# A selective-state kernel: growth factors and dt's steps in PSUM, C rotated on GpSimd, the MLP sum earlier on VectorE, and the products from the states over all four heads at a time

## What is computed

```python
zxbcdt = x @ in_proj_w.T                        # z, x, B, C and dt; x is layer-normalised first
dt  = softplus(zxbcdt[..., -NHEADS:] + dt_bias)
xBC = silu(causal_conv4(xBC))                   # x_ssm (4 heads x 64), B and C (32 complex each)
theta      = clip(theta_base + tanh(x @ theta_w1) @ theta_w2)
lambda_eff = lambda_base + eta * theta ** 2
log_z  = complex(-lambda_eff * dt, theta * dt)
x_disc = x_ssm * dt
# linear recurrence over time, for every head and state k:
#   S_t = exp(log_z_t) * S_{t-1} + B_t * x_disc_t ;   y_t = Re(sum_k C_t * S_t)
y = y + x_ssm * D
g = rmsnorm(y * silu(z)) * norm_w
out = x + g @ out_proj_w.T + mlp(layernorm(x))  # 128 -> 512 -> 512 -> 128, weights +1 and -1
```

## Time and profile before

| | |
|---|---|
| median of 3 runs | 410.99 us (410.89 to 411.18) |
| profiled execution | 410.37 us, span of its instructions 407.0 us |
| TensorE busy | 334.8 us, 82% |
| VectorE busy | 310.3 us, 76% |
| ScalarE busy | 171.7 us, 42% |
| GpSimd busy | 147.6 us, 36% |
| mean granted TensorE clock | 0.94 of full speed |

### The profile page before, as it was taken

One profiled execution on the slowest core, in us unless ns is written; L12 is line 12 of the kernel. 1 busy time (PEld: TensorE's weight loads), 2 busy tenths in 40 slices (PEclk: granted clock), 3 DMA queues, 4 the chain that ended last, 5 costly groups with the idle time before them and its releaser, 6 DMA issues.

```text
span 407.0 us, 9993 instructions
## 1 busy us (share of the span) xinstructions
PE 334.8 (82%) x3962; PEld 234.9 (58%) x3962; DVE 310.3 (76%) x655; ACT 171.7 (42%) x305; POOL 147.6 (36%) x124
## 2 busy tenths in 40 slices
PE   0469289889979997989979997999799997895582
PEld 0444146577657664776567765766477655752571
DVE  2695789688968897789958896889868994888221
ACT  0307643375317714473427531771447343651020
POOL 1001077107621465107810762136610880076301
PEclk9999579999989999999989998999989998998896
DMA  7101200320023001400031002300040003000001
GB/s 192 15 0 40 64 0 2 81 52 2 27 61 73 2 0 42 108 14 0 27 84 48 2 27 62 73 2 2 26 122 11 0 27 85 23 2 26 2 2 31
DMA packets 19097, 14.86 MB, mean 36 GB/s; under 512 B 5045, under 2 KB 14826, under 8 KB 19050
## 3 DMA queue, kind: packets, MB, share of 16 engines
q1 hardware_dynamic: 16090, 13.67, 12.8%
q10 hardware_dynamic: 2960, 0.49, 0.7%
HBM read 3.67 MB, written 2.10 MB: 14 GB/s over the span
## 4 chain that ended last, share of the span: by engine, by line
DVE 47%; PE 26%; issue 11%; ACT 10%; POOL 2%; DMA 2%; SPq 1%; DVEq 1%; ACTq 0%; POOLq 0%
PE bank L1329 6%; PE bank L1420 4%; DVE h1l L723 3%; PE bank L1397 3%; DVE tmpd L614 3%; PE bank L1281 2%; DVE xd L539 2%; DVE phl L554 2%; DVE tmpc L613 2%; PE bank L1339 2%; DVE cum L586 2%; DVE ds L521 2%; DVE dacc L525 2%; DVE osb L736 2%; ACT z L970 2%
## 5 line engine op out<-in xcount | busy, mean ns | idle before, releaser
L1310 PE MATMUL bank<-h0h,W 128*128 128x512 f16 x128 | 50.3, 393 | 4.7 <-DVE h1l L723 3.2
L1160 POOL TENSOR_TENSOR btmp<-Kre,bres 128x512 f32<-128x512 f32 x8 | 8.5, 1059 | 125.5 <-DVE Kim L604 125.5
L1311 PE MATMUL bank<-h0l,W 128*128 128x512 f16 x128 | 50.1, 392 | 0.0
L1262 PE MATMUL bank<-XW,xh 128*128 128x256 f16 x256 | 49.1, 280 | 0.0
L1113 POOL TENSOR_TENSOR rstd<-vare,minus_half 128x4 f32<-128x4 f32 x8 | 8.1, 1018 | 77.0 <-DVE negmean L501 77.0
L1262 PE MATMUL bank<-XW,xl 128*128 128x256 f16 x128 | 35.7, 279 | 0.0
L1329 PE MATMUL bank<-Ure,Kre 32*128 32x128 f32 x256 | 20.3, 395 | 17.1 <-DVE o L727 12.8
L658 DVE TENSOR_TENSOR GT<-bank,const 128x512 f32<-128x512 f32 x32 | 19.9, 683 | 14.0 <-PE bank L1339 13.9
L1262 PEld LDWEIGHTS bank<-XW,xh 128*128 128x128 f16 x256 | 25.5, 100 | 7.1 <-issue 0.4
L938 ACT ACTIVATE de<-dneg 128x16 f32<-128x16 f32 x8 | 1.7, 216 | 65.2 <-DVE dneg L514 65.2
L1329 PEld LDWEIGHTS bank<-Ure,Kre 32*128 32x128 f32 x256 | 16.2, 287 | 20.6 <-issue 18.1
(11 more groups left out here) (193 smaller groups left out, 989.6 us busy)
## 6 DMA issues: line engine op xcount, KB each, us to landing
xtok<-in_x SPq DMA_DIRECT2D x8, 256.0 KB, 3.1
cres<-bc SPq DMA_DIRECT2D x32, 64.0 KB, 2.2
cims<-bc SPq DMA_DIRECT2D x32, 64.0 KB, 2.3
bres<-bc SPq DMA_DIRECT2D x32, 64.0 KB, 2.1
bims<-bc SPq DMA_DIRECT2D x32, 64.0 KB, 2.1
out<-osb SPq DMA_DIRECT2D x8, 256.0 KB, 2.3
const<-constants SPq DMA_DIRECT2D x1, 576.0 KB, 5.6
KT<-in_in_proj_w SPq DMA_DIRECT2D x1, 320.0 KB
```

Source lines behind the costliest of these rows:

```text
L1262: last = M.matmul(dst, tok(x, c, k), w[:, k, :], start=False, stop=(k == TAPS - 1 and q == 2))
L1310: M.matmul(bank[4 + f % 2][:], w, h0h[:, k, :], start=(k == 0), stop=False)
L1311: last = M.matmul(bank[4 + f % 2][:], w, h0l[:, k, :], start=False, stop=(k == MT - 1))
```

## The change

- `lz` is written over bank 2 (which held the spread dt), and the scan reads it there. The transposes of the next input, which write bank 2, wait for the scan (`PHASE_STEPS + 2`) where they waited for `lz`.
- Both exponentials go to bank 3 (`growth`), one after the other: exp(-c) for K, then, once K is made (`s_kq.at(n, 2)`), exp(c). `lora1`, which writes bank 3, waits for the last product with it.
- dt's intermediate values lie in bank 1 behind dt's projection (dv, dneg, dsum, dq, dacc), so that every VectorE instruction of the chain has at most one tensor input in SBUF; two instructions are added (a copy dvs of dv, a copy dr of the quotient): 16 instead of 14. TensorE's U by K products, which write bank 1, wait for the whole chain of n+1 (`s_dt.done(n)`) instead of its first step.
- Q was C (ec, es) in eight VectorE instructions. Now GpSimd rotates C by the phases alone (`c_rotated`: R = C pcs, psn; six instructions, started by the cosine and the repeated C), VectorE makes Q = R growth in two (`decayed(1)`). U was Q B in six GpSimd instructions; now GpSimd makes R B (`b_times_rotated`, six), VectorE U = R B growth in two (`decayed(2)`).
- GpSimd's order: roots, `c_rotated`, root for the RMS norm, `b_times_rotated`, `b_and_k(0)`, `b_and_k(1)`.
- VectorE's order behind `decayed(1)`: `h1_low(0)`, `final`, `h1_low(1)`, `dt_input`, `x_times_dt`, `dt_steps`, `h1_low(2)`, `decayed(2)`, `h1_low(3)`, `add_mlp`, `largest`.
- `from_state` runs over all four heads for each chunk, and both gates are released by the last of them.
- SP's repeat of B's rows waits for `s_bk` in place of `s_u`.

```diff
+        lz, growth = bank[2], bank[3]
             def decayed(n, part):
                 step = chain(s_kq, n)
-                if part < 2:
-                    e_and_k(n, step, part)
-                    return
-                step.count[0] = 3 * part - 2
-                if part == 2:
-                    v.wait_ge(c_in.sem, c_in.done(n))
-                    wait_past(s_u, n)
-                    rotated(step, part, Qre[:], (cres[:], ec[:]), (cims[:], es[:]), ALU.subtract, False)
+                step.count[0] = 2 * part
+                if part == 0:
+                    v.wait_ge(a_trig.sem, a_trig.done(n))
+                    v.wait_ge(a_exp.sem, a_exp.at(n, 1))
+                elif part == 1:
+                    v.wait_ge(a_exp.sem, a_exp.at(n, 2))
+                    v.wait_ge(s_rot.sem, s_rot.done(n))
                 else:
-                    rotated(step, part, Qim[:], (cres[:], es[:]), (cims[:], ec[:]), ALU.add, True)
+                    v.wait_ge(s_v.sem, s_v.done(n))
+                for dst, src in (((Kre, pcs), (Kim, psn)), ((Qre, Rre[:]), (Qim, Rim[:])), ((Ure, Ure[:]), (Uim, Uim[:])))[part]:
+                    step(V.tensor_tensor(dst[:], src, growth[:], ALU.mult), linked=False)
@@ VectorE, pipelined
                 if has_front:
                     decayed(n, 1)
                     h1_low(n, 0)
-                    decayed(n, 2)
+                if has_back:
+                    final(n - 1, pq, stored)
+                if has_front:
                     h1_low(n, 1)
-                    decayed(n, 3)
                 if next_loaded is not None:
                     dt_input(n + 1)
-                if has_back:
-                    final(n - 1, pq, stored)
-                if has_front:
-                    h1_low(n, 2)
-                    h1_low(n, 3)
+                if has_front:
                     x_times_dt(n, p)
                 if next_loaded is not None:
                     dt_steps(n + 1)
                 if has_front:
+                    h1_low(n, 2)
+                    decayed(n, 2)
+                    h1_low(n, 3)
                     add_mlp(n, p)
                     largest(n)
@@ GpSimd
+            def turned(sig, n, re, im, left):
+                (a, b), (c, d) = left
+                for k, (dst, f1, f2, op) in enumerate(((re, c, d, ALU.subtract), (im, d, c, ALU.add))):
+                    P.tensor_tensor(btmp[0][:], a[:], f1, ALU.mult).then_inc(sig.sem, 1)
+                    P.tensor_tensor(btmp[1][:], b[:], f2, ALU.mult).then_inc(sig.sem, 1)
+                    g.wait_ge(sig.sem, sig.at(n, 3 * k + 2))
+                    P.tensor_tensor(dst[:], btmp[0][:], btmp[1][:], op).then_inc(sig.sem, 1)
+                    g.wait_ge(sig.sem, sig.at(n, 3 * k + 3))
+            def c_rotated(n):
+                g.wait_ge(c_in.sem, c_in.done(n))
+                g.wait_ge(a_trig.sem, a_trig.done(n))
+                turned(s_rot, n, Rre, Rim, ((cres, cims), (pcs, psn)))
+            def b_times_rotated(n):
+                g.wait_ge(b_in.sem, b_in.done(n))
+                turned(s_v, n, Ure, Uim, ((bres, bims), (Rre[:], Rim[:])))
                 if has_front:
-                    b_and_k(n, s_kq, 0)
+                    c_rotated(n)
                 if has_back:
                     rms_of(n - 1)
                 if has_front:
+                    b_times_rotated(n)
+                    b_and_k(n, s_kq, 0)
                     b_and_k(n, s_kq, 1)
-                    u_products(n)
@@ TensorE
             def xn_transposed(n):
-                    pe.wait_ge(s_ph.sem, s_ph.at(n - 1, PHASE_STEPS + 1))
+                    pe.wait_ge(s_ph.sem, s_ph.at(n - 1, PHASE_STEPS + 2))
@@ pipelined
-                        pe.wait_ge(s_dt.sem, s_dt.at(n, 1))
-                    pe.wait_ge(s_u.sem, s_u.done(b))
+                        pe.wait_ge(s_dt.sem, s_dt.done(n))
+                    pe.wait_ge(s_kq.sem, s_kq.done(b))
@@
-                    for heads in ((0, 1), (2, 3)):
-                        for j in range(1, NCH):
-                            last = from_state(b, True, j, heads)
-                        last.then_inc(t_y.sem, 1)
+                    for j in range(1, NCH):
+                        last = from_state(b, True, j, range(HEADS))
+                    last.then_inc(t_y.sem, 2)
```

More of the change, by code:

```diff
@@ L285, in build @@
         s_xl = signal("xn_low_half", 1)
-        s_dt = signal("dt_steps", 9 + len(ATANH))
+        s_dt = signal("dt_steps", 11 + len(ATANH))
         s_xd = signal("x_times_dt", 1)
@@ L289, in build @@
         s_tail = Level(ctx, nc, "K_exponents", 1)
-        s_kq = signal("decayed", 4 + 6)
+        s_kq = signal("decayed", 2 + 2 + 2)
         s_kqg = Level(ctx, nc, "decayed_general", 4 + 12)
@@ L320, in build @@
         c_in = signal("C_repeated", 2 * HEADS * 16)
-        s_u = signal("U_products", 6)
+        s_rot = signal("C_rotated", 6)
+        s_v = signal("B_times_rotated", 6)
         s_cb = Level(ctx, nc, "B_times_C", 6)
@@ L385, in build @@
         sums_in = bank[1][:, 256:256 + NCH]
-        dt_in = bank[1][:, 288:288 + NCH * HEADS]
+        dt_in, dv, dneg, dsum, dq, dacc = (
+            bank[1][:, 288 + NCH * HEADS * k:288 + NCH * HEADS * (k + 1)].rearrange("p (c h) -> p c h", h=HEADS) for k in range(6))
+        lz, growth = bank[2], bank[3]
         tap_bank = [bank[k] for k in (0, 1, 7, 3)]
@@ L516, in dt_steps @@
+                step(V.scalar_tensor_tensor(dneg[:], dv[:], -1.0, dvs[:], ALU.mult, ALU.min), linked=False)
             def dt_steps(n):
                 step = chain(s_dt, n)
-                step.count[0] = 2
+                step.count[0] = 3
                 v.wait_ge(a_dte.sem, a_dte.done(n))
-                step(V.tensor_scalar(ds[:], de[:], 2.0, None, ALU.add))
-                step(V.reciprocal(dq[:], ds[:]))
-                step(V.tensor_tensor(ds[:], de[:], dq[:], ALU.mult))
-                step(V.tensor_tensor(dq[:], ds[:], ds[:], ALU.mult))
@@ L525, in dt_steps @@
-                step(V.tensor_scalar(dacc[:], dq[:], ATANH[-1], None, ALU.mult))
+                step(V.tensor_scalar(dsum[:], de[:], 2.0, None, ALU.add))
+                step(V.reciprocal(dq[:], dsum[:]))
+                step(V.tensor_tensor(dr[:], de[:], dq[:], ALU.mult), linked=False)
+                step(V.tensor_tensor(dsum[:], de[:], dq[:], ALU.mult))
+                step(V.tensor_tensor(dr2[:], dr[:], dsum[:], ALU.mult))
+                step(V.tensor_scalar(dacc[:], dr2[:], ATANH[-1], None, ALU.mult))
@@ L532, in wait_past @@
+                step(V.scalar_tensor_tensor(dacc[:], dacc[:], 1.0, dr[:], ALU.add, ALU.mult), linked=False)
+                step(V.tensor_scalar(dmax[:], dv[:], 0.0, None, ALU.max))
+                step(V.scalar_tensor_tensor(dt[:], dacc[:], 2.0, dmax[:], ALU.mult, ALU.add))
             def wait_past(sig, n):
@@ L780, in pipelined @@
                     h1_low(n, 0)
-                    decayed(n, 2)
-                    h1_low(n, 1)
-                    decayed(n, 3)
-                if next_loaded is not None:
-                    dt_input(n + 1)
                 if has_back:
@@ L788, in pipelined @@
                 if has_front:
-                    h1_low(n, 2)
-                    h1_low(n, 3)
+                    h1_low(n, 1)
+                if next_loaded is not None:
+                    dt_input(n + 1)
+                if has_front:
                     x_times_dt(n, p)
@@ L993, in decays @@
                         act.wait_ge(s_ph.sem, s_ph.done(n))
-                        step(a_exp, A.activation(E[:], cum3[:, 0, :], ACT.Exp, scale=-1.0))
+                        step(a_exp, A.activation(growth[:], cum3[:, 0, :], ACT.Exp, scale=-1.0))
                     else:
@@ L999, in decays @@
                     return
-                step(a_exp, A.activation(E2[:], cum3[:, 0, :], ACT.Exp))
+                if fast:
+                    act.wait_ge(s_kq.sem, s_kq.at(n, 2))
+                step(a_exp, A.activation(growth[:] if fast else E2[:], cum3[:, 0, :], ACT.Exp))
                 if fast:
@@ L1240, in dt_products, with lora1 @@
                     for k, (x, w) in enumerate(pairs(DTW)):
-                        last = M.matmul(dt_in[:, HEADS * c:HEADS * c + HEADS], tok(x, c), w[:], start=(k == 0), stop=(k == 2))
+                        last = M.matmul(dt_in[:, c, :], tok(x, c), w[:], start=(k == 0), stop=(k == 2))
                 last.then_inc(t_dt.sem, 1)
-            def lora1(n):
+            def lora1(n, fast):
                 if not (isinstance(n, int) and n == 0):
                     pe.wait_ge(a_th.sem, a_th.at(n, 0))
+                    pe.wait_ge(s_kq.sem, s_kq.at(n, 0) if fast else s_kq.done(SEQS - 1))
                 for k, (x, w) in enumerate(pairs(TW1)):
```

45 lines of the change are left out of this document (15 added, 30 removed).

## The result

| | before | changed |
|---|---|---|
| median, us | 410.94 (4 runs, 410.82 to 411.18) | 390.75 (4 runs, 386.86 to 392.08) |
| profiled execution, us | 410.37 | 389.54 |
| its span, us | 407.0 | 387.3 |
| mean granted clock | 0.941 | 0.942 |

The ratio is 0.9492, with a 95% interval of 0.9419 to 0.9566: 20.2 us less, where the forecast had 15.5. Lines of the changed kernel stand 3 to 15 lower in the file: L1344 is L1329 of before, L1354 is L1339, L1435 is L1420, L1412 is L1397, L1334 is L1319, L1246 is L1232, L732 is L727 and L591 is L587.

The account below looks back on a forecast made before the run. The prediction took TensorE, waiting for VectorE's late MLP sum and then slowed by half clock, as the bound. Terms of -14.7, -2.7, -9.4, +3.8, -0.3 and +7.8 sum to -15.5: 394.9 profiled, 395.5 us median, range 386 to 404.5.

Parts of the forecast that it names:

- Waits: TensorE's waits before the MLP's output and U by K go, the last front step counted apart: -14.7 us.
- The clock at L1344: With little idle ahead, U by K runs at full clock, six times 1.57 us gained: -9.4 us.
- The clip: VectorE's clip waits for a GpSimd product of C's rotation, 0.47 us in each of eight steps: +3.8 us.
- The rival without shield by PSUM: K, Q or the scan is held by C's rotation despite PSUM operands, 1.1 us in eight steps: 404.3 us; 7%.
- Four heads: The 48 products from the states take about 1.3 us instead of 2.4: worth 0, at n = 8 -0.3 us.
- The last front step: With no next sequence, U by K starts at 375.7 to 377.2 instead of 379.88: -2.7 us.
- The lower clock moves: Idle around the transposes brings half clock to output projection and MLP in five of seven steps: +7.8 us.
- the clock stays up: Rival, 20%: the idles around the transposes leave the clock at 1.00, so 7.8 us isn't paid: 387.7 us.
- The case that would have made it slower: GpSimd's path through U to `h1_low(3)`, with 1.1 us of slack, could be 4.3 us late: 418 us; 5%.

Follow-up runs that it names:

- the late rotation: The changed kernel with C's rotation held on GpSimd until the clip is done: 388.82 us, ratio 0.9476.
- the fills in the kernel before: The kernel before with five unread matmuls of 512 columns between the LoRA product and the wait for the MLP sum: 404.4 us, ratio 0.9863.

## Why the prediction was right, and where it was off

**Waits: right.** The sum behind `h1_low(3)` takes the waits away, nothing took their place at L1344 (the sum is 2.5 us early, as worked out), and GpSimd's path was fast enough, with a slack that the late rotation puts nearer to 2 us than to the 1.1 worked out. That this move alone bears nearly all of the result (390.24 us and 0.9522, where the changed kernel has 390.75 and 387.99, 0.9492 and 0.9465) the prediction didn't say. It is shown by the run with the moved line.

**The clock at L1344: right, a little too large.** All of n = 2 to 7 take 2.07. The forecast took one row, 3.64, for all six; by their own rows they gave back 8.6 us, not 9.4. That the slow stretch is caused by idle ahead of it and not by L1329 itself is shown by the fills in the kernel before. They also show that this gain needed the sum off VectorE's chain.

**The clip: right.** 0.86 us against 0.43, +0.43 where 0.47 was worked out; in the prologue 1.52. The rival without shield by PSUM fell: K, Q, U, scan and gates keep their times, and lose them with both inputs in SBUF.

**Four heads: right on the overlap** (1.55 us for 48, not 2.46; the two heads that share a bank write different columns of the array) and on its being worth nothing; at n = 8 the products begin and the output projection follows 0.31 us sooner, as forecast.

**The last front step: about right.** 39.18 us against 41.89. Without the 1.4 us that L1435 lost to the lower clock there (3.47 us, not 2.05) it is 4.1 less, and the terms for this step, -2.7, the clock's 1.0 (its L1329 took 3.08) and the clip's 0.5, give 3.2. The step also had a stretch at half clock before the change, from 369.6 to 373.0; now one of 10 us begins at 352.3, over the MLP's output (3.59 us for 1.96), which the forecast had allowed for.

**"The lower clock moves": the mis-sized term.** I took five of seven stretches, 7.8 us. The profiled execution has one of seven (n = 7, 1.4 us), that of the same kernel run again two (n = 1 and 7). What was added elsewhere in the first: 2.2 us from the start of the last L1344 on, and 1.3 in the prologue. There the stretch at half clock is 13.7 us long in both kernels, but it ends at 58.8 instead of 55.5 and so covers more of MLP layer 1; what follows is 1.9 us late, of which 0.6 was there ahead of it. The idle in the loop was as forecast, 2.1 us around the transposes. What it does to the clock isn't fixed by it: the same two idles, to 0.1 us, went with none and one slow output projection in the six loop steps of the changed kernel, four in the one with a filled prologue and three with the exponentials in SBUF. What decides it stays open. In n = 7 the idle is one of 2.72 us, which the forecast didn't see apart; where it is 2.2 us or more, L1435 is slow there in six traces of seven, and in none of the three traces of this kernel's variants where it is 0.1 to 1.8. The rival "the clock stays up" (387.7) had the mechanism, and the median of 390.75 lies between it and the forecast.

**Not in the sum.** By terms: -14.7 waits, -8.6 clock, -2.7 last step, -0.3 at n = 8, +3.1 clip in n = 1 to 7 (6 x 0.43 and 0.49), +1.8 prologue (0.6 later, and the 1.27 us of wait that should have made it earlier), +1.4 and +2.2 lower clock at n = 7 and 8, +0.3 behind TensorE's last instruction. That is -17.5, with -19.7 measured on the span. Of the 2.2 us that are left 1.4 lie in the six loop steps, 0.24 in each: L1334 follows L1435 0.43 to 0.53 us sooner than before, though the wait listed there was 0.27 to 0.36, and L1344 gains 0.07 more than its wait. A wait thus costs a little more than its listed idle. The other 0.8 is in the last front step, of which the forecast took only the end. The 1.1 us outside the span has no row.

The case that would have made it slower, GpSimd as the bound, is not far: the collision of `x_times_dt` lasts 2.13 us as before, and a rotation 2.5 us later already brought waits of 0.4 us per step; in the last front step GpSimd is the bound now.

## What to carry to other kernels

Find the instruction whose semaphore the bounding engine waits for, and look at what is queued ahead of it that nobody waits for; here one line moved was worth 19 us, and the rest of the change 0 to 2 more. Short instructions from SBUF to SBUF on VectorE can each wait out a GpSimd product when GpSimd is kept busy beside them, so moving work to GpSimd and moving VectorE's small operands to PSUM belong together. An idle of TensorE costs its length and then, sometimes, half of the speed of what follows; count the second part as a spread, not as a sum.

## What the runs showed of the hardware that I had not expected

- Thirteen instructions of 16 elements took 9.5 us beside GpSimd's products, and 2.54 beside the same products with an operand of each in PSUM.
- Identical idles of TensorE (0.97 and 1.12 us) were followed by 1.00 or by half clock, from step to step and from execution to execution; a slow output projection took 1.1 to 1.6 us more than its 2.05. Six executions of one kernel spread over 8 us (387.8 to 395.8), with mean clocks from 0.965 to 0.942.
- TensorE stands 0.9 to 1.3 us at the start of two of the loop's passes, for no other engine. In the three kernels with matmuls added in the prologue a second such gap, 0.7 to 1.4 us, stood in the middle of U by K; nine added in the loop alone brought none. None of the runs says what it is.
- Where a VectorE product with both inputs in SBUF lasted 1.76 us beside GpSimd, GpSimd's own products were longer as well: 1.75 and 1.60 us instead of 1.27.
